# One signal per routed tile, per half of a shared block and per pair of norm transposes

## What is computed

```python
# first block
n1 = layernorm(x)
Bu = einsum('sd,bld->lbs', B, n1)            # 64 states
h  = scan: h_t = a * h_{t-1} + Bu_t          # over the 512 tokens of a batch
x1 = x + einsum('ds,lbs->bld', C, h) + D * n1
# second block
n2 = layernorm(x1)
shared = (silu(n2 @ shared_gate.T) * (n2 @ shared_up.T)) @ shared_down.T      # hidden width 256
top_id = argmax(n2 @ gate_w.T)                # one of 8 experts for each token
score  = sigmoid(max(n2 @ gate_w.T))
routed = (silu(xs @ r_gate[top_id].T) * (xs @ r_up[top_id].T)) @ r_down[top_id].T,  xs = n2 * score
out = x1 + shared + routed
```

## Time and profile before

| | |
|---|---|
| median of 3 runs | 302.53 us |
| profiled execution, its own time | 304.56 us |
| its span (first to last instruction) | 302.5 us |
| PE busy | 242.1 us (80%) |
| DVE busy | 185.1 us (61%) |
| ACT busy | 169.0 us (56%) |
| POOL busy | 143.9 us (48%) |
| mean granted clock of TensorE | 0.913 |

### The profile page before, as it was taken

One profiled execution on the slowest core, in us unless ns is written; L12 is line 12 of the kernel. 1 busy time (PEld: TensorE's weight loads), 2 busy tenths in 40 slices (PEclk: granted clock), 3 DMA queues, 4 the chain that ended last, 5 costly groups with the idle time before them and its releaser, 6 DMA issues.

```text
span 302.5 us, 6183 instructions
## 1 busy us (share of the span) xinstructions
PE 242.1 (80%) x1891; PEld 184.7 (61%) x1891; DVE 185.1 (61%) x594; ACT 169.0 (56%) x411; POOL 143.9 (48%) x148
## 2 busy tenths in 40 slices
PE   0776959768796399995999718999999999998930
PEld 0355636446465157663767506999999999975720
DVE  4799967899986756559684103556555556543400
ACT  2927798896885741321223328777767666642410
POOL 1000000037775004776787600577777777777570
PEclk9998778999799579999799955999999999999995
DMA  7999000002222001328512366055464644311193
GB/s 237 400 325 397 3 0 3 0 33 107 102 104 89 2 0 37 109 108 274 193 72 107 109 199 231 29 161 161 126 196 143 175 131 124 105 50 54 30 157 47
DMA packets 23806, 37.30 MB, mean 123 GB/s; under 512 B 3648, under 2 KB 15808, under 8 KB 23216
## 3 DMA queue, kind: packets, MB, share of 16 engines
q1 hardware_dynamic: 15264, 22.03, 23.8%
q0 software_dynamic: 8512, 14.89, 16.9%
HBM read 22.03 MB, written 19.20 MB: 136 GB/s over the span
## 4 chain that ended last, share of the span: by engine, by line
PE 34%; issue 19%; POOL 16%; DVE 13%; ACT 11%; DMA 3%; SPq 0%; POOLq 0%; ACTq 0%
POOL table L990 13%; PE bank L446 11%; PE bank L434 6%; PE bank L436 5%; PE bank L435 5%; ACT n L539 4%; PE bank L407 3%; POOL out L1038 3%; ACT rows L553 3%; DVE stats L681 2%; DVE stats L712 2%; ACT w_split L571 2%; DVE h L701 1%; DVE rows L708 1%; DMA rows<-in_x 1%
## 5 line engine op out<-in xcount | busy, mean ns | idle before, releaser
L990 POOL DMA_INDIRECT table<-rows,place x64 | 66.0, 1032 | 88.0 <-DVE place L770 46.5
L1031 POOL DMA_INDIRECT out<-w_full x51 | 49.4, 969 | 34.1 <-DVE w_full L966 19.2
L599 ACT ACTIVATE n1T<-bank,g_scale 128x512 f32<-128x512 f32 x32 | 22.0, 687 | 46.6 <-PE bank L388 40.5
L434 PE MATMUL bank<-xT_hi,w_split 128*128 128x256 f16 (+1 forms) x156 | 41.9, 271 | 0.2
L436 PE MATMUL bank<-xT_hi,w_split 128*128 128x256 f16 (+1 forms) x156 | 41.9, 271 | 0.0
L435 PE MATMUL bank<-xT_lo,w_split 128*128 128x256 f16 (+1 forms) x156 | 41.8, 270 | 0.0
L446 PE MATMUL bank<-w_full,hid 128*128 x284 | 38.5, 277 | 0.1
L446 PEld LDWEIGHTS bank<-w_full,hid 128*128 128x128 f32 x284 | 34.8, 192 | 1.4 <-issue 0.2
L918 DVE SCALAR_TENSOR_TENSOR hid<-bank,h_scale,n1T 128x512 f32<-128x512 f32 x32 | 23.5, 747 | 18.6 <-ACT n1T L599 13.1
L400 PEld LDWEIGHTS bank<-w_full,hid 128*128 128x128 f32 x256 | 31.8, 197 | 2.1 <-issue 0.3
L400 PE MATMUL bank<-w_full,hid 128*128 128x128 f32 x256 | 31.9, 280 | 0.0
(11 more groups left out here) (136 smaller groups left out, 440.9 us busy)
## 6 DMA issues: line engine op xcount, KB each, us to landing
w_full<-table SPq DMA_DIRECT2D x24, 264.0 KB, 3.3
rows<-in_x SPq DMA_DIRECT2D x8, 512.0 KB, 7.6
w_full<-in_weights SPq DMA_DIRECT2D x3, 1152.0 KB, 11.6
table<-in_pads SPq DMA_DIRECT2D x1, 2112.0 KB, 8.6
table<-in_pads SPq DMA_DIRECT2D x8, 264.0 KB
x_ring<-table SPq DMA_DIRECT2D x8, 264.0 KB, 3.2
out<-rows POOLq DMA_DIRECT2D x6, 256.0 KB, 6.7
table<-rows,place POOLq DMA_INDIRECT x64, 2.4
```

Source lines behind the costliest of these rows:

```text
L434: mm(o, w_of(kind, e, 0, c), xT_hi[k][:, 0:w], start=True, stop=False)
L990: g.indirect_dma_start(table[:, :], bass.IndirectOffsetOnAxis(ap=place[:, i:i + 1], axis=0), rows[:, i, :], None).then_inc(done, 16)
L1031: g.indirect_dma_start(out[:, :], bass.IndirectOffsetOnAxis(ap=x_in[k][:, s, 2 * D:2 * D + 1].bitcast(I32), axis=0), x_in[k][:, s, 0:D], N ...
```

## The change

PE raises fewer semaphores, and what waited for a part now waits for the whole group:

- Norm stage: one signal for both halves of transpose_n1, one for both halves of transpose_n2. The second half of transpose_n2(s-1) is moved ahead of y(s). Both copies of the first norm, and both split_hi, wait for that one signal.
- Shared stage: gate c and up c of a block share one signal, so shared_silu(c) waits for up c too.
- Routed stage: PE raises `r_pe` once at the end of routed_gate_up(j), which covers the transposes of tile j+2 and the second layer of tile j-3 that stand ahead of it. tile_hi, tile_lo, routed_silu, routed_hidden and routed_result all wait for that one number. routed_down is now three iterations behind (`BEHIND = 3`) and stands at the start of an iteration, where routed_down(j-2) stood at the end. The routed weights' registers are five instead of three.
- What is computed, and each instruction of each engine, stays the same.

The core of the diff:

```diff
             def transpose_n1(q):
...
                     for t in range(BT):
                         last = nc.tensor.transpose(bank[b][:, P * t:P * (t + 1)], n1[:, BT * b + t, :], identity)
-                    last.then_inc(s_t1, 1)
+                last.then_inc(s_t1, 1)
...
             for s in range(-1, PAIRS):
                 if s >= 1:
-                    transpose_n2(s - 1, 0)
+                    transpose_n2(s - 1)
                 if s >= 0:
                     y(s)
-                if s >= 1:
-                    transpose_n2(s - 1, 1)
...
+        def turned(j):
+            return max(j, 1)
+        def gated(j):
+            return j + 2
+        def downed(j):
+            return j + BEHIND + 2
...
             for j in range(TILES):
+                if j == BEHIND:
+                    pe.wait_ge(s_late, MIDDLE)
+                if j >= BEHIND:
+                    routed_down(j - BEHIND)
                 if j + 2 < TILES:
                     transpose_tile(j + 2)
-                routed_gate_up(j)
-                if j == 0:
-                    pe.wait_ge(s_late, MIDDLE)
-                if j >= 2:
-                    routed_down(j - 2)
+                routed_gate_up(j).then_inc(r_pe, 1)
                 if j + 1 < TILES:
                     load_expert(j + 1)
...
             def copy_n1T(q, b):
-                act.wait_ge(s_t1, q * 2 + b + 1)
+                act.wait_ge(s_t1, q + 1)
...
             def shared_silu(s, c):
-                act.wait_ge(s_g, s + 1)
+                act.wait_ge(s_gu, s + 1)
...
             def tile_hi(j):
-                act.wait_ge(s_xt, j + 1)
-                after(act, r_u, j - XTRING + 1)
+                act.wait_ge(r_pe, turned(j))
...
             def routed_silu(j):
-                act.wait_ge(r_g, j + 1)
+                act.wait_ge(r_pe, gated(j))
...
             def routed_result(j):
-                dve.wait_ge(r_o, j + 1)
+                dve.wait_ge(r_pe, downed(j))
...
             for j in range(-2, TILES):
+                if j >= BEHIND:
+                    routed_result(j - BEHIND)
                 if j + 2 < TILES:
                     tile_lo(j + 2)
-                if j >= 2:
-                    routed_result(j - 2)
                 if j >= 0:
                     routed_hidden(j)
```

More of the change, by code:

```diff
@@ L332, in y, with transpose_n2 @@
                 last.then_inc(s_y, 1)
[L334 to L339, removed]
+            def transpose_n2(q):
+                for b in range(2):
+                    pe.wait_ge(s_n2, q * 2 + b + 1)
+                    after(pe, s_lo, q * 2 + b - 1)
+                    for t in range(BT):
+                        i = q * PT + BT * b + t
+                        last = nc.tensor.transpose(bank[5 + b][:, P * t:P * (t + 1)], n2[:, i, :], identity)
                 last.then_inc(s_t2, 1)
@@ L382, in shared_gate_up @@
                     f = slice(P * c, P * (c + 1))
-                    for kind, banks, used, done in ((0, gate_bank, s_silu, s_g), (1, up_bank, s_hid, s_u)):
+                    for kind, banks, used in ((0, gate_bank, s_silu), (1, up_bank, s_hid)):
                         after(pe, used, b * FC + (c - FC + 1))
@@ L387, in shared_gate_up @@
                         mm(o, w_split[:, 0, kind, 0, f], n2T_lo[:, tok], start=False, stop=False)
-                        mm(o, w_split[:, 1, kind, 0, f], n2T_hi[:, tok], start=False, stop=True).then_inc(done, 1)
+                        last = mm(o, w_split[:, 1, kind, 0, f], n2T_hi[:, tok], start=False, stop=True)
+                    last.then_inc(s_gu, 1)
             def shared_down(b):
@@ L405, in transpose_tile @@
                 after(pe, s_xl, j - 1)
+                last = None
                 for s in range(halves(j)):
                     last = nc.tensor.transpose(tile_bank[j % 2][:, P * s:P * (s + 1)], x_in[j % XRING][:, s, D:2 * D], identity)
-                last.then_inc(s_xt, 1)
+                return last
             w_flat = w_split[:].rearrange("p h k e f -> p (h k e f)")
-            expert_reg = [nc.tensor.alloc_register(f"expert{k}") for k in range(3)]
+            expert_reg = [nc.tensor.alloc_register(f"expert{k}") for k in range(BEHIND + 2)]
             def load_expert(j):
-                nc.tensor.reg_load(expert_reg[j % 3], tile_weights[0:1, j:j + 1])
+                nc.tensor.reg_load(expert_reg[j % (BEHIND + 2)], tile_weights[0:1, j:j + 1])
             def down_of(j, c):
@@ L429, in routed_gate_up @@
                 e = expert(j)
-                for kind, banks, used, done in ((0, gate_bank, r_silu, r_g), (1, up_bank, r_hid, r_u)):
+                for kind, banks, used in ((0, gate_bank, r_silu), (1, up_bank, r_hid)):
                     after(pe, used, j - 1)
@@ L436, in routed_gate_up @@
                         last = mm(o, w_of(kind, e, 1, c), xT_hi[k][:, 0:w], start=False, stop=True)
-                    last.then_inc(done, 1)
+                return last
             def routed_down(j):
@@ L446, in routed_down @@
                         last = mm(o, hid[j % 4][:, slot], down_of(j, c), start=(c == 0), stop=(c == FC - 1))
-                last.then_inc(r_o, 1)
+                return last
             pe.wait_ge(s_const, 16)
@@ L477, in _ @@
                 if b == 0:
-                    transpose_n2(LAST, 0)
-                    transpose_n2(LAST, 1)
+                    transpose_n2(LAST)
                 if b == 1:
@@ L536, in norm1 @@
                 act.wait_ge(s_nb1, q + 1)
-                after(act, s_t1, q * 2)
+                after(act, s_t1, q)
                 for t in range(PT):
@@ L948, in tile_lo @@
                 dve.wait_ge(s_xh, j + 1)
-                after(dve, r_u, j - XTRING + 1)
+                dve.wait_ge(r_pe, turned(j))
                 w = width(j)
@@ L970, in _ @@
             for j in range(-2, TILES):
+                if j >= BEHIND:
+                    routed_result(j - BEHIND)
                 if j + 2 < TILES:
                     tile_lo(j + 2)
-                if j >= 2:
-                    routed_result(j - 2)
                 if j >= 0:
                     routed_hidden(j)
-            routed_result(TILES - 2)
-            routed_result(TILES - 1)
+            for j in range(TILES - BEHIND, TILES):
+                routed_result(j)
             for b in range(FIRST, BLOCKS):
```

33 lines of the change are left out of this document (17 added, 16 removed).

## The result

The changed kernel is slower: 312.50 us (median of 4 runs, 311.62 to 313.35) against 303.44 us for the kernel before (4 runs, 301.9 to 304.5). The ratio is 1.0296, 95% interval 1.0257 to 1.0335, that is 9.1 us more. Its profiled execution took 313.01 us with a span of 311.0, against 304.56 and 302.5. The times of one kernel vary by up to 4 us from execution to execution.

What follows compares the result with a forecast made beforehand. POOL's gapless row of 71 result scatters sets the end, so delays before the first result count in full. Norm stage 5.4 plus routed stage 1.8 us, added to 302.5, gave 309.7 us; range 306 to 313.

Steps and rivals of the forecast that it cites:

- the three signs of being wrong: Trace checks: residual(7) moves under 3 us, gaps in POOL's result row, or PE matmuls closer than 0.11 us.
- Fewer signals: All stages on PE: 161 fewer signals gain 0 us, at most 1.6 us if all of PE were on the path.
- y behind the whole of norm2: Norm stage: y waits for all of norm2(s-1), adding 1.3, 0.97 and 1.54 us in pairs 1, 5 and 7.
- the chain of 5.04 us: Norm stage, norm2(s-1) to residual(s): norm2 3.19, signal 0.06, transposes to y 0.58, y to residual 1.21 us.
- Pair 6 at 0: Norm stage: y waits for the scan, which ends after norm2(5) and its transposes, so no cost.
- TensorE falls to 1.2 GHz more often: Rival, norm stage and first gates: PE idles longer, work costs double, 3 to 4 us more, 313 us; chance 0.14.
- Copies behind both halves: Norm stage, ACT: n1's first copy waits for both halves, 0.95 and 0.62 us to pairs 2 and 3, hidden elsewhere.
- Norm stage, sum: Norm stage: y and copy delays make residual(7) 5.4 us late, and everything to the first result moves with it.
- Routed stage: First result in the routed stage: 0.31 us for tile_hi plus 1.49 for the second layer's signal, together 1.8 us.
- the late signal: Routed stage: tile 0's second layer signals only after tile 5's transposes and tile 3's gate and up, 1.49 us.
- the place behind the product: Routed stage, DVE: tile 2's product ahead of the first result might delay it; counted only in the 2.8 us upper bound.
- Shared stage and the rest of the routed stage, 0: Later silu, tile_hi and products cost 0 us, covered by other PE work and POOL's 3.66 us backlog.

Runs made afterwards that it cites:

- run 5: Changed kernel with the 161 saved signals raised again at their old places, on a semaphore nobody waits for: 312.69 us, ratio 1.033 to the kernel before.
- run 9: Kernel before with only the norm stage's edits, both merged signals and the move of the second transposes ahead of y: ratio 1.0258, +7.8 us.
- run 2: Kernel before with one signal for both halves of transpose_n1 and nothing else: 307.31 us, ratio 1.013.
- run 6: Changed kernel with y put back between the two halves of transpose_n2, still one signal for both: 308.99 us, ratio 1.0201 to the kernel before.
- run 1: Kernel before with only the second half of transpose_n2(s-1) moved ahead of y(s), each half keeping its signal: 310.40 us, ratio 1.0256.
- run 3: Kernel before with one signal for gate and up of each half of a shared block, nothing else: 303.55 us, ratio 1.0000.
- run 4: Changed kernel's routed stage alone, norm and shared stages as in the kernel before: 305.66 us, ratio 1.008 to the kernel before.
- run 7: Changed kernel's routed stage alone on the kernel before, but the second layer raises its own signal at once; result still behind the product: 305.61 us, ratio 1.0087.
- run 8: Kernel before with the routed second layer one iteration behind instead of two, and the result behind the product on DVE: 301.84 us, ratio 0.9964.
- run 10: Kernel before with the changed routed stage, but the second layer signals at once and the result stands ahead of the product on DVE: 304.09 us, ratio 1.0011.
- run 11: Kernel before with y(s) ahead of both halves of the transposes of n2: 303.02 us, ratio 0.9969.
- run 12: Kernel before with y ahead of both n2 transposes, routed second layer one iteration behind, result behind the product: 301.62 us, ratio 0.9921.

## Why the prediction was right, and where it wasn't

The predicted 309.7 us lies 2.8 below the measured 312.5, inside the range of 306 to 313 but near its end. 0.9 of it is the kernel before, whose median over four runs is 303.4. In the profiled executions, against which the sum was made, the span went up by 8.5, not by 7.2.

The mechanism is the one named: none of the three signs of being wrong appeared (residual(7) moved by 7.54 us and not by less than 3, POOL's row kept 1.274 us a scatter, PE's matmuls kept 0.11 us). But the number is nearer than its parts. I had put the move at 3.8 us and the copies at 1.6; measured alone they are 7.8 and 3.9, and only because the two overlap is the norm stage 7.8 us instead of 11.7. That part is luck.

**Fewer signals, 0.** Right; PE's pace in run 5 shows it.

**y behind the whole of norm2.** Right in place and in size for pairs 5 and 7: 0.98 and 1.54 us added, 0.97 and 1.54 predicted. PE's timeline around pair 7 (L350 transposes, L340 y):

```profile
99.78 0.64 PE L350 MATMUL bank<-const,rows 128*128 128x128 f32 x4
100.80 0.66 PE L350 MATMUL bank<-const,rows 128*128 128x128 f32 x4 [0.38 <-ACT rows L564]
101.39 1.16 PE L340 MATMUL bank<-const,h 64*128 64x128 f32 x16
```

The second half waits for ACT, which ends norm2(6) at 97.56 + 3.19 = 100.75; 0.05 us later the transposes start, y 0.59 behind them, residual 1.21 behind y: the chain of 5.04 us, measured as 102.60 - 97.56 = 5.04. Pair 1 was mis-sized: 1.72 instead of 1.3. I had chosen between 0.5 and 1.75 by the clock. The granted clock is 0.63 over these transposes and 0.50, which is 1.2 GHz, over all of y:

```profile
29.06 0.93 PE L350 MATMUL bank<-const,rows 128*128 128x128 f32 x4 [0.88 <-ACT rows L564]
29.91 2.08 PE L340 MATMUL bank<-const,h 64*128 64x128 f32 x16
```

y takes 2.08 us where it takes 1.16 at 2.4 GHz; so the slow end of the bound was the right one.

**Pair 6 at 0.** Here norm2(5) does end ahead of the scan (86.19 + 3.19 = 89.38, scan until 89.00 + 1.22 = 90.22), and y starts at 90.36, 0.14 behind the scan. But the step cost 0.71, since y ran at a granted clock of 0.61 and took 1.77 us instead of 1.16; that is 0.61 of it. The transposes of n1 behind it ran at 1.2 GHz too:

```profile
90.36 1.77 PE L340 MATMUL bank<-const,h 64*128 64x128 f32 x16
92.06 1.97 PE L317 MATMUL bank<-const,n 128*128 128x128 f32 x8
```

The eight transposes took 1.97 us, where they took 1.33 before at full clock, but this cost nothing: from residual(6) to norm2(6) it is 5.39 us, against 5.38. The trace of run 9 has the same code in this stage, and there pair 6 costs 98.52 - 87.78 = 10.74 us against 91.56 - 80.90 = 10.66 before, so nothing, but pair 5 costs 1.27 more than here. PE of run 9 at pair 5 (L340 transposes, L330 y):

```profile
79.32 1.01 PE L340 MATMUL bank<-const,rows 128*128 128x128 f32 x4 [0.88 <-ACT rows L551]
80.26 2.08 PE L330 MATMUL bank<-const,h 64*128 64x128 f32 x16
```

So this is the rival "TensorE falls to 1.2 GHz more often", for one pair of eight. It is a part of the miss, and not a fixed property of pair 5 or 6.

**Copies behind both halves.** 0.97 and 0.70 in pairs 2 and 3, 0.95 and 0.62 predicted. What failed is "in the other steps ACT then waits for DVE all the same, and this hides it". It isn't so in pair 5, where the copies cost 0.70 us in runs 2 and 6; in the changed kernel this lies beside y's 0.97 and adds nothing. And it isn't so in pair 0, the start of the whole chain, where nothing runs that could hide it. ACT's first copy and DVE's first scan, before:

```profile
10.95 0.57 ACT L547 ACTIVATE n1T<-bank 128x512 f32<-128x512 f32 x1
```

```profile
14.48 1.22 DVE L701 TENSOR_TENSOR_SCAN h<-const,bank 128x512 f32<-128x512 f32 x1 [0.53 <-PE bank L314]
```

and in the changed kernel:

```profile
12.23 1.09 ACT L558 ACTIVATE n1T<-bank 128x512 f32<-128x512 f32 x2 [0.99 <-PE bank L317]
```

```profile
15.37 1.22 DVE L711 TENSOR_TENSOR_SCAN h<-const,bank 128x512 f32<-128x512 f32 x1 [1.23 <-PE bank L324]
```

The first copy waits 0.99 us for the second half of the transposes, and DVE 1.23 us for what follows from it. Between these two traces pair 0 is 0.89 late. The start of this pair also varies a little by itself: norm2(0) begins at 24.93 to 25.43 in the profiles of runs that leave the copies alone (the kernel before, runs 1, 3, 4, 7, 8, 10, 11, 12) and at 25.82 to 25.99 in those that have the edit (the changed kernel, runs 2, 5, 6, 9). I take some 0.7 us for it, between 25.82 - 25.43 = 0.4 and 25.99 - 24.93 = 1.1. This is the largest term that the sum lacked.

**Norm stage, sum.** 5.4 predicted; 7.54 at residual(7) (102.60 - 95.06). Of the 2.1 more, 0.89 is the first pair, 0.42 pair 1, and 0.71 the clock in pair 6. The first shared scatter is only 6.29 later. The stretch between the two took 21.92 us before and 20.67 after. Over the profiles of kernels whose code is the same there as before, it took 20.4 (run 4) to 21.9 us (run 8), so these 1.25 us lie within the spread between executions and are no gain of the change. That they bring the sum back towards the predicted one is luck too.

**Routed stage.** 1.8 predicted. In the trace 1.49 (199.57 - 123.27 = 76.30 against 74.81); by the times 2.4 alone and 1.3 within the whole. Over all profiles this stretch is 74.2 to 74.8 us with the routed stage of before (the kernel before, runs 1, 2, 3, 9, 11) and 75.6 to 76.3 with the new one (the changed kernel, runs 4, 5, 6, 7). The first part, 0.31 for tile_hi, is there: the first gates start 2.98 us behind the first transposes (189.83 - 186.85) and started 2.61 behind them before (183.21 - 180.60), 0.37 more. The second part, 1.49 for the late signal, was only half the story. DVE of the changed kernel, product of tile 2 (L968) and first result (L975):

```profile
198.08 0.75 DVE L968 SCALAR_TENSOR_TENSOR hid<-bank,h_scale,n1T 128x512 f32<-128x512 f32 x1 [0.80 <-ACT n1T L649]
198.87 0.42 DVE L975 TENSOR_TENSOR w_full<-bank,w_full 128x256 f32<-128x256 f32 x1
```

and PE, with the second layer of tile 0, the transposes of tile 5, and the first and the last matmul of gate and up 3:

```profile
196.15 1.15 PE L459 MATMUL bank<-w_full,hid 128*128 x8 [0.15 <-issue]
197.14 0.38 PE L420 MATMUL bank<-const,w_full 128*128 128x128 f32 x2
197.36 0.27 PE L447 MATMUL bank<-xT_hi,w_split 128*128 128x256 f16 x1
...
198.56 0.27 PE L449 MATMUL bank<-xT_hi,w_split 128*128 128x256 f16 x1
```

The group's last matmul ends at 198.56 + 0.27 = 198.83. The product ends at 198.08 + 0.75 = 198.83. In run 7, without the wait for the group, the result started 0.67 us behind the start of the product; that would be 198.75 here, against the 198.87 of the trace. So the two waits end within 0.12 us. The one that I named was real, but the one that I kept for the upper bound, the place behind the product, stood beside it at nearly its full size: taking away the first alone gives nothing (run 7), taking away both gives 1.5 to 2.3 us (run 10). No run takes away the place alone.

**Shared stage and the rest of the routed stage, 0.** Right: run 3, and the row of 71 scatters at 1.274 us.

**What stays open.** The move alone measured 7.8 us and the move inside the changed kernel 3.0. In the profiled executions the norm edits overlap by 1 to 2 us and not by the 3.9 of the times: residual(7) is late by 5.3 in run 1, by 4.15 in run 2, together 9.4, and by 8.5 (run 9) and 7.5 (the changed kernel) with both. The overlap can be seen where both edits delay the same pair: 0.98 and 0.70 alone in pair 5, 0.98 together; 0.38 and 0.70 in pair 3, 0.70 together. The rest seems to be the unprofiled executions of run 1 (309.87 to 311.8, profiled 309.0), which are slow by 1 to 3 us. The mean granted clock of the four goes down as the time goes up (0.919, 0.919, 0.913 and 0.903 for 309.0, 309.87, 310.93 and 311.8 us); a clock that falls in one or two more pairs would be such a sum (up to 1.3 us each), but no trace of these executions shows it. Open too is why run 8's first result, 3.6 us earlier in its trace, brought 1.0 us by the medians; part of it is that the one profiled execution of the kernel before (304.56 us) was 0.9 to 1.7 us above the medians of its runs.

## What to carry to other kernels

A signal that a matmul raises costs PE nothing that can be seen here, but whoever waits for a merged signal pays the time between its own piece and the last of the group: count this at each place that no other wait covers, the pipeline's first round above all. Before you blame a wait, look at what stands ahead of the waiting instruction on its own engine, since two waits that end together hide each other in any experiment that removes one. And work that needs nothing of the previous step, such as y, must not be queued behind work that does.

## What I had not expected of the hardware

The same instructions in the same order run at 2.4 GHz in one execution and at 1.2 in another. PE in the changed kernel at pair 5:

```profile
77.46 0.66 PE L350 MATMUL bank<-const,rows 128*128 128x128 f32 x4 [0.64 <-ACT rows L564]
79.00 0.66 PE L350 MATMUL bank<-const,rows 128*128 128x128 f32 x4 [0.89 <-ACT rows L564]
79.59 1.16 PE L340 MATMUL bank<-const,h 64*128 64x128 f32 x16
```

y takes 1.16 us here and 2.08 in run 9, with the same code; in pair 6 it is the other way round, 1.77 here and 1.16 there. PE had idled nearly alike ahead of pair 5's second transposes in both, 0.64 and 0.89 us here, 0.63 and 0.88 there. One such fall cost 0.6 us (y of pair 6 here) and 1.3 (pair 5 in run 9). The two kernels are alike in the norm stage and differ behind it; why the clock falls in one pair or another, no run here shows. In the profiles of the kernels whose norm stage is as before, residual(7) starts anywhere from 95.06 (the kernel before) to 96.78 (run 3), so a sum of waits in a stage where TensorE keeps stopping can't be checked on one profiled execution to better than 1 to 2 us.
